# First expert combination joined with the attention projection; third parts on GpSimd

## The reference

```python
# layer 0, experts: y_e = relu(xn @ W1[e] + b1[e]) @ W2[e] + b2[e]
x = x + tanh(g_ffn[0]) * sum_k gate[:, k] * y[expert_k]          # combination 0
# layer 1, attention
xn = layernorm(x)
q, k, v = xn @ Wq.T, xn @ Wk.T, xn @ Wv.T                       # 16 heads of 16
att = softmax(q @ [ctx_k, k].T / 4) @ [ctx_v, v]
x = x + tanh(g_xattn[1]) * (att @ Wproj.T + b_proj)
# layer 1, experts: silu(xn @ W1[e]) * (xn @ W3[e]) @ W2[e], top 4 of 32
out = x + tanh(g_ffn[1]) * sum_k gate[:, k] * y[expert_k]        # combination 1
```

## Time and profile before

| | us |
|---|---|
| median of three runs | 1393.61 |
| the profiled execution, its time | 1405.55 |
| the profiled execution, its span | 1403.8 |
| PE, DVE, ACT, POOL busy in the span | 1138.9, 759.5, 587.4, 329.7 |
| `experts0` | 102 to 400 |
| `combine(0)` | 400.2 to 424.2 |
| `project_qkv` | 425.3 to 493.3 |
| `attend` | 493.6 to 962.8 |
| `combine(1)` | 1307.1 to 1403.8 |

### The profile page before, as it was taken

How to read it: one execution, slowest core, us unless ns; L and a number is a source line. 1 busy time by engine, 2 the same in 40 slices (tenths; PEclk the granted TensorE clock), 3 DMA queues, 4 the chain that set the end, 5 groups by cost and what they waited for, 6 DMA issues and landing times. The chain is left out here.

```text
span 1403.8 us, 27582 instructions
## 1 busy us (share of the span) xinstructions
PE 1138.9 (81%) x6985; PEld 742.8 (53%) x6986; DVE 759.5 (54%) x2074; ACT 587.4 (42%) x1391; POOL 329.7 (23%) x534
## 2 busy tenths in 40 slices
PE   4849999999926879999999999987439999999100
PEld 3749999999913412333233233324418888888100
DVE  6552222222244687888788888822684555555432
ACT  3622221222214406777677777775343333333000
POOL 2012222222106032111101101010003333332565
PEclk9959999999957958999999999999658999999655
DMA  5365455555347533303203123000107888888333
GB/s 176 122 222 180 174 175 185 184 186 185 111 126 184 159 73 48 39 11 49 39 10 48 20 29 48 1 1 17 44 10 233 252 255 257 251 252 249 97 107 114
DMA packets 135332, 172.73 MB, mean 123 GB/s; under 512 B 17574, under 2 KB 112800, under 8 KB 135130
## 3 DMA queue, kind: packets, MB, share of 16 engines
q1 hardware_dynamic: 119786, 132.46, 33.9%
q0 software_dynamic: 13168, 37.37, 9.4%
q10 hardware_dynamic: 2304, 2.10, 0.4%
HBM read 141.29 MB, written 30.38 MB: 122 GB/s over the span
## 5 line engine op out<-in xcount | busy, mean ns | idle before, releaser
L1953 DVE TENSOR_REDUCE arena<-ps 128x1 f32<-128x512 f32 x512 | 327.5, 682 | 73.5 <-PE ps L1794 67.0
L1924 ACT ACTIVATE arena<-ps 128x512 f32<-128x512 f32 (+1 forms) x576 | 304.4, 598 | 142.7 <-PE ps L1835 141.0
L1835 PE MATMUL ps<-arena 99*128 99x512 bf16 (+1 forms) x576 | 217.2, 389 | 6.0 <-ACT arena L1924 5.5
L1794 PE MATMUL ps<-arena 96*128 96x512 bf16 x512 | 206.7, 407 | 13.7 <-DMA arena<-k_parts 11.4
L895 POOL DMA_INDIRECT xg<-xn,tcol x134 | 127.7, 953 | 340.3 <-DVE tcol L928 338.5
L1824 PE MATMUL ps<-arena 128*17 128x512 f32 (+1 forms) x1152 | 154.4, 608 | 2.1 <-ACT arena L1924 1.0
L1835 PEld LDWEIGHTS ps<-arena 99*128 99x128 bf16 (+1 forms) x576 | 57.1, 101 | 180.4 <-ACT arena L1924 139.1
L1144 PE MATMUL ps<-scratch,arena 128*128 128x128 f32 x1140 | 148.4, 280 | 4.4 <-DMA arena<-in_L_ffn_w 2.3
L986 PEld LDWEIGHTS ps<-scratch,arena 128*128 128x128 f32 x1248 | 147.6, 194 | 3.6 <-issue 1.7
L986 PE MATMUL ps<-scratch,arena 128*128 128x128 f32 x1248 | 148.0, 278 | 1.1 <-ACT scratch L1017 1.1
L1144 PEld LDWEIGHTS ps<-scratch,arena 128*128 128x128 f32 x1140 | 136.3, 194 | 12.0 <-issue 10.7
(11 more groups left out here) (309 smaller groups left out, 1258.6 us busy)
## 6 DMA issues: line engine op xcount, KB each, us to landing
arena<-in_L_ffn_W SPq DMA_DIRECT2D x47, 1024.0 KB, 5.0
arena<-in_L_ffn_w SPq DMA_DIRECT2D x190, 192.0 KB
y<-ysb SPq DMA_DIRECT2D x95, 128.0 KB
arena<-k_parts SPq DMA_DIRECT2D x48, 137.6 KB, 4.9
arena<-q_parts SPq DMA_DIRECT2D x96, 64.0 KB, 5.2
scratch<-y SPq DMA_DIRECT2D x16, 256.0 KB
arena<-in_L_ffn_w POOLq DMA_DIRECT2D x8, 512.0 KB, 10.9
xg<-xn,tcol POOLq DMA_INDIRECT x134
```

The source lines that it names most:

```text
L1794: nc.tensor.matmul(ps[:, MAXB + pos % NMAXB, :], e.q_aug[u][0:QROWS, c, h, t * P:(t + 1) * P], e.k_aug[u][0:QROWS, h, CL + k * HB:CL + (k ...
L1835: nc.tensor.matmul(ps[0:rows, SB + n % NSB, :], e.k_aug[u][0:AROWS, h, k0:k0 + rows], e.q_aug[u][0:AROWS, c, h, :], start=True, stop=True) ...
L1924: nc.scalar.activation(e.prob[s % 2][0:rows, h, :], ps[0:rows, SB + (s * GH + h) % NSB, :], ACT.Exp).then_inc(p_ready, 1)
L1953: v.tensor_reduce(e.mx[:, c, h, t, k:k + 1], ps[:, MAXB + pos % NMAXB, :], AX.X, ALU.max).then_inc(max_done, 1)
```

## The change

Five things, in one diff. (1) `combine(0)` is gone as a stage: `combine_and_project` does its work inside the projection's block, chunk by chunk (`combined(c)`: four tiles combined, statistics, scale and shift of these four tiles), with all 16 loads issued at once into 16 buffers (`YG0`), and the weights' transposes at the head of PE and ACT. The clearing of the semaphores now stands behind `experts0`. (2) The third parts are made by POOL. (3) The 16 loads of `load_w2` and the clearing of the padding move from POOL in the projection to SP's end and POOL's beginning in `attend`, since the new buffers lie where these weights go. (4) `load_group(0)` is issued after the stores of chunk 1 and a wait for the stores of chunks 0 and 1. (5) `combine1` has 16 tile buffers and no ring, no register loops on DVE and ACT, and adds tile by tile where pairs were.

```diff
-def combine(e, layer):
+def combine1(e):
...
+    yg = e.carve(0, [NTILE, kk, D])
...
+        @block.gpsimd
+        def _(pool):
+            for i in range(NTILE):
+                for k in range(kk):
+                    pool.indirect_dma_start(out=yg[:, i, k, :], out_offset=None, in_=e.y[1],
...
+            for i in range(NTILE):
                 for k in range(kk):
...
+                    if k == 0:
+                        dve.wait_ge(got[i], 16 * kk)
+                    else:
+                        dve.wait_ge(step, i * (kk - 1) + k)
+                    v.scalar_tensor_tensor(e.x[:, i, :], yg[:, i, k, :], e.gate[:, i, k:k + 1], e.x[:, i, :],
+                                           ALU.mult, ALU.add).then_inc(step if k < kk - 1 else added, 1)
...
-def project_qkv(e):
+def combine_and_project(e):
...
-            for ex in range(0, E1, W2_TURN):
-                load_w2(e, pool, ex)
-            nc.gpsimd.memset(e.w2b[IB:IB_PAD, :, 1, :], 0.0)
+            def third_parts(c, w):
+
+                for n in range(4):
+                    pool.wait_ge(part1, (c + 1) * 4 + n + 1)
+                    nc.gpsimd.tensor_tensor(e.parts[c % 2][:, n, 2, 0:w], e.left[:, n, 0:w], e.parts[c % 2][:, n, 1, 0:w], ALU.subtract).then_inc(unit_done, 1)
+
+            third_parts(-1, CL)
+            for c in range(CH):
+                third_parts(c, HB)
 
         @block.sync
         def _(sp):
+            y = e.y[0][0:NTOK * kk, :].rearrange("(k i p) d -> p i k d", k=kk, p=P)
+            for i in range(NTILE):
+                sp.dma_start(yg[:, i, :, :], y[:, i, :, :]).then_inc(got[i], 16)
...
-                if c * HB == S:
+                if (c + 1) * HB == S:
                     for n in range(4):
-                        sp.wait_ge(stored[(c - 1) % 2][n], 16 * ((c + 1) // 2 + 1))
+                        sp.wait_ge(stored[0][n], 16 * (c // 2 + 1))
+                        sp.wait_ge(stored[1][n], 16 * (1 + (c + 1) // 2))
                     load_group(e, sp, 0, 0)
...
             def norm(c):
+                act.wait_ge(var_ready, c + 1)
+                nc.scalar.activation(e.std[:, c * CHUNK:(c + 1) * CHUNK], e.ve[:, c * CHUNK:(c + 1) * CHUNK], ACT.Sqrt).then_inc(std_ready, 1)
+                act.wait_ge(shift_ready, c + 1)
...
-            values(0)
-            left(-1, CL)
-            third_parts(-1, CL)
+            combined(0)
+            left(-1, CL)
+            combined(1)
+            values(0)
             for c in range(CH):
+                if c + 2 < CH:
+                    combined(c + 2)
                 left(c, HB)
                 if c + 1 < CH:
                     values(c + 1)
-                third_parts(c, HB)
...
             groups(sp, body)
+            for ex in range(0, E1, W2_TURN):
+                load_w2(e, sp, ex)
```

More of the change, by code:

```diff
@@ L58 @@
 ZN_AT = 32768
+YG0 = 32768
 E1_SCRATCH = 2 * 4 * D * 4
@@ L1230, in _ @@
                 out(j, j % RING1, j // RING1)
-def combine(e, layer):
+def combine1(e):
     nc, sem = e.nc, e.sem
[L1236 to L1244, removed]
-    with nc.Block() as block:
[L1247 to L1272, removed]
+    kk = K1
+    got = [sem(f"co1_got{i}") for i in range(NTILE)]
+    step, added, stored, weight_step = sem("co1_step"), sem("co1_added"), sem("co1_stored"), sem("co1_weight_step")
+    yg = e.carve(0, [NTILE, kk, D])
+    o = NTILE * kk * D * 4
+    scores = e.carve(o, [kk, NTILE * E1]); o += kk * NTILE * E1 * 4
+    w = e.carve(o, [NTILE, kk]); o += NTILE * kk * 4
+    tot = e.carve(o, [NTILE])
+    with nc.Block() as block:
+        @block.gpsimd
[3 more added lines that the diff above has]
+                    pool.indirect_dma_start(out=yg[:, i, k, :], out_offset=None, in_=e.y[1],
+                                            in_offset=bass.IndirectOffsetOnAxis(ap=e.slot_u[:, i, k:k + 1], axis=0)).then_inc(got[i], 16)
         @block.vector
@@ L1329, in combine @@
-        if last_layer:
-            @block.scalar
-            def _(act):
-                o = e.out.rearrange("b (t p) d -> p (b t) d", p=P)
-                with act.Fori(0, NTILE) as i:
-                    act.wait_ge(added, i + 1)
-                    act.dma_start(o[:, i, :], e.x[:, i, :]).then_inc(stored, 16)
-                act.wait_ge(stored, 16 * NTILE)
+            ch = Chain(dve, weight_step)
+            for k in range(kk):
+                ins = v.tensor_tensor(scores[:, k].rearrange("p (i e) -> p i e", e=E1), e.chosen[:, k], e.sig, ALU.mult)
@@ L1339, in attention_buffers, with _ @@
+        @block.scalar
+        def _(act):
+            o = e.out.rearrange("b (t p) d -> p (b t) d", p=P)
+            for i in range(NTILE):
+                act.wait_ge(added, i + 1)
+                act.dma_start(o[:, i, :], e.x[:, i, :]).then_inc(stored, 16)
+            act.wait_ge(stored, 16 * NTILE)
 def attention_buffers(e):
@@ L1393, in project_qkv @@
     XB, VB, UB = 0, 2, 4
+    kk = K0
+    got = [sem(f"qkv_got{i}") for i in range(NTILE)]
+    summed, added = sem("qkv_summed"), sem("qkv_added")
+    yg = e.carve(YG0, [NTILE, kk, D])
+    wturn = later_turns(e)
+    w_raw, w_done = sem("qkv_w_raw"), sem("qkv_w_done")
+    NTR = 4
     with nc.Block() as block:
@@ L1521, in left @@
                                            ALU.mult, ALU.subtract).then_inc(left1, 1)
-            def third_parts(c, w):
-                for n in range(4):
-                    dve.wait_ge(part1, (c + 1) * 4 + n + 1)
-                    v.tensor_tensor(e.parts[c % 2][:, n, 2, 0:w], e.left[:, n, 0:w], e.parts[c % 2][:, n, 1, 0:w], ALU.subtract).then_inc(unit_done, 1)
             def values(c):
```

95 lines of the change are left out of this document (39 added, 56 removed).

## The result

The changed kernel takes 1377.49 us (median of 4 runs, 1377.17 to 1378.54) against 1396.96 us for the kernel before (4 runs, 1392.65 to 1401.02): ratio 0.9859, 95% interval 0.9826 to 0.9891. I had forecast 1372.7 us and a range of 1362 to 1389, a gain of 20.9 us. On another chip, with more runs, the ratio is 0.9884 (0.9853 to 0.9914), 1379.94 against 1395.73 us. So the gain is 19.5 us on the first chip and 15.8 on the other.

The account below looks back on a forecast made before the run. No single engine bounds it: each block waits for its own slowest chain. Head 13.4 plus last combination 7.5 gave 20.9 us off the profiled 1405.55, 1384.7, carried over as a difference to 1372.7 us on 1393.61; range 1362 to 1389.

Parts of the forecast that it names:

- Start of the block, first chunk: Projection's block starts at 401.2, POOL's clearing beside DVE costs 1.5 us, normalising starts at 412.2, 18.4 us earlier.
- The new wait: DVE's queue in the projection: PE waits from about 418 until 423.5; first units at 428.5 instead of 442.99.
- Chunks 1 and 2: Projection: PE's values of chunk 2 start at 457.4, about 6 us late; chunk 3's units end at 476.
- Third parts on POOL: Projection: 1.29 us each (bounds 0.72 and 1.44); at the end, last chain ends 6.4 us behind PE's last unit.
- Loads: First group's loads ready at 481.3, just ahead of block's end; rival: attention waits until about 490, 1378, chance 0.06.
- Clock: Projection: PE's new gap of 8 us before chunk 2 costs 3 to 4 us at low clock, 2 us net.
- Port: SBUF port in the projection, while POOL reads: DVE's combined(3) loses 1 us, bounds 0 and 5.2 us.
- Attention keeps its length: Attention, starting at 484.5 instead of 497.91, begins with DVE's maxima as the limit and takes as long as before.
- Last combination: Last combination: POOL does not pause, last tile's adds and store end sooner; 8.1 us, taken as 7.5 us.
- port lock: Rival in the projection, chance 0.08: combined(3) waits for all third parts of chunk 0, 5.2 us instead of 1; 1377.
- pause absent: Rival in the last combination, chance 0.22: POOL's pause is not in ordinary runs, so only 1 us gained; 1379.
- Low clock throughout: Rival in the projection, chance 0.08: PE at 1.2 GHz from first unit to last, attention starts near 516.5; 1405.

Follow-up runs that it names:

- new orders: Changed kernel with other queue orders on PE, ACT and DVE in the merged block: 1374.67 us, 0.9838 of the kernel before.
- late loads: Changed kernel with the 18 loads of attention's first group back behind chunk 2's stores: 1381.95 us, 0.9889 of the kernel before.
- split end: Kernel with the new orders, two of the last chunk's four third parts made by DVE, two by POOL: 1375.84 us, 0.9801 of the kernel before.

## Why the prediction was right, and where its sizes were off

- *Start of the block, first chunk.* Right. First add at 406.09 (block start + 4.4), normalising at 412.06 (said 412.2), DVE held by the clearing as said. The block itself started at 401.8, 0.6 later than I had it, and the steps behind it took that much less.
- *The new wait.* Right, to 0.1 us: units at 428.43 (said 428.5). They ran at full clock, so they ended 1.7 us sooner than I had.
- *Chunks 1 and 2.* The gap ahead of chunk 2 is there, values at 454.88 (said 457.4), last units end at 477.4 (said 476). That 476 was near is luck: my own terms, 457.4 + 3.62 + 7.03 and the distance of 10.67, give 478.7, and nothing in the rows justified taking 476. The values started 2.5 us sooner than I had and took 1.4 longer, and the distance was 10.67. The new orders, which close the gap, started attention 4.4 us sooner.
- *Third parts on POOL.* 1.12 us against my estimate of 1.29, inside the bounds 0.72 and 1.44. The tail behind PE's last unit is 5.7 us (477.4 to 483.1), said 6.4. Putting them on DVE again showed that the move is worth next to nothing by itself.
- *Loads.* Hidden as said; late loads cost 2.4 us of the start. The rival in which they limit is out.
- *Clock.* The term of 2 us was about right in kind and a little too large. The clock is 1.00 in the gap ahead of chunk 2 itself and falls right behind it; window of the changed kernel:

```profile
454.80:457.00 2.20, 2.20 (x7) 1.77 (x6) 0.17 (x1) 2.16 (x6) 0.90 (x1) 0.50 0.00 0
```

  The values of chunk 2 took 4.98 us where the same 16 matmuls took 3.62 in chunk 1: 1.4 us. In other traces of the same code it was 1.2 (the changed kernel again) and 2.5 (with 20 memsets). The units behind ran at 7.03 us as before. Attention starts at 483.47; I had said 484.5, where 482.4 + 0.3 + 2 is 484.7.
- *Port.* I took 1 us, measured 1.29 for two adds. It is not hidden: `combined(3)` ends at 449.6, ACT, which has waited 7.95 us for this chunk's statistics before its square root, starts normalising at 449.68, behind the end of PE's units at 448.9, and the values of chunk 2 wait for what follows; so it is part of the gap ahead of chunk 2. The trace agrees with the rule of the Trainium skill (SBUF — State Buffer, Who interferes with whom) that a DVE instruction with two SBUF inputs contends with a GpSimd instruction that reads SBUF: 2.15 us for two adds beside POOL's reads and 0.86 without, and both engines slower in the split end. My rival of 5.2 us had DVE waiting for all four third parts. POOL had started them at 439.61 and was done at 444.29, and DVE's first adds came at 442.42, so only two adds met them; and had both waited for POOL's end, they would have ended at 445.16, where they ended at 444.57. So one of them ran before POOL was done.
- *Attention keeps its length.* This is a step that failed. It was 3.1 us shorter in the trace, for a stretch of low clock that it did not have; and the experiments show lengths between 462 and 474 us, by such stretches (3 to 4 us each) and by DVE's gaps at the turns of the loop, neither of which my steps looked at. That the change did not come out 10 us worse, as it does with 20 idle memsets, is luck.
- *Last combination.* The term was mis-sized: 9.5 us in the trace for my 7.5. The pause gave what I said, but the gathers got shorter by 1.0 us besides; the end behind the last gather became 2.2 us shorter where I had 1.7, and POOL's own end, for which I had taken 0.6 off, cost nothing. By medians it is 7.6.
- *From the profile to the median.* The sum over the traces was 28.2, I had 20.9: 7.3 too little. The 11.94 us by which before's profiled execution stood above its median I carried over as a difference, and the changed kernel's execution stands at its median: 11.9 too much. The two partly cancel and leave 4.8 us between 1372.7 and 1377.49: that the forecast is this near is luck in part. What those 11.94 us were stays open: before's runs spread over 8 to 13 us on every chip, the changed kernel's over 1.4 and 5.3, and I have only one trace of the kernel before.
- *The rivals.* The measured 1377.49 lies nearer to the numbers of three rivals (port lock 1377, loads 1378, pause absent 1379) than to my 1372.7. Their mechanisms are not in the runs: two adds waited 1.29 us and not 5.2, attention's first matmul is released by the barrier and not by the loads, and the new last combination alone gains 7.6 us. Low clock throughout did not come either: the units took 7.03 us.

## What to carry to other kernels

When one engine's work stands whole in front of a stage, deal it out by chunks to the stage, and then look at each queue for what stands ahead of what is wanted first: here the order alone was worth another 5 us of the median. A profiled execution above its median is not to be carried over as a difference without asking which rows hold the excess. Before a change is judged by some microseconds, see whether a loop elsewhere has changed its length: move its code by some idle instructions and time it again.

## What the runs showed of the hardware that was not expected

- With 20 more instructions ahead of a register loop DVE issues nothing for 5.0 to 5.2 us behind the first instruction of each of two turns; with none, one or 40 more it does not. PE waits 2.7 to 3.9 us for it, and its matmuls behind the wait take 0.61 us instead of 0.38. With 20 idle memsets the kernel is 9.9 us slower by the median. The kernel before showed none of this at the two places tried.
- The same matmuls of attention run at 1.00 or, for 7 to 9 us, at about 0.6 at a turn of the loop, from one variant to the next, with nothing changed in attention: 3.4 us.
- POOL's subtraction of 128x512 takes 1.12 us, less than twice the 721 ns for 256 elements of the earlier trace rows.
- Two two-input instructions on DVE and two on POOL at once take 1.14 and 1.36 us each, alone 0.62 and 1.12: from the start of the first to the end of the last it is 3.26 us, where one behind the other would be 3.48.
